# Attention features on two halves of 64 partitions, two heads in one pass of the array, and DRAM rows ordered by batch

## What is computed

```python
scores = einsum('bhqd,bhkd->bhqk', q, k) / sqrt(8)   # + bias, by core
attn = softmax(scores, axis=-1)
out = einsum('bhqk,bhkd->bhqd', attn, v)
```

## Time and profile before

| | |
|---|---|
| runs | 1136.57, 1138.33, 1139.11 us, median 1138.33 |
| profiled execution | span 1137.3 us from its first instruction to its last; no time of its own is given beside the span |
| busy | TensorE 866.6 us (76%), weight loads 548.7 (48%), DVE 652.5 (57%), ScalarE 517.1 (45%), GpSimd 155.7 (14%) |
| DMA | 80.82 MB in 109103 packets, 105280 of them under 2 KB; HBM read 49.61 MB, written 29.82 MB |
| chain that ended last | TensorE 62%, DVE 11%, DMA 7%, SyncE's queue 6%, issue 5% |

### The profile page before, as it was taken

The page is one execution under the profiler, slowest core; times in us unless marked ns, Lnnn a source line. Parts: engine busy times, 40 slices in busy tenths (PEclk is TensorE's granted clock), DMA queues, the critical chain, the costliest instruction groups (busy, mean ns, idle before and its releaser), DMA issues.

```text
span 1137.3 us, 21997 instructions
## 1 busy us (share of the span) xinstructions
PE 866.6 (76%) x7183; PEld 548.7 (48%) x7205; DVE 652.5 (57%) x1690; ACT 517.1 (45%) x867; POOL 155.7 (14%) x170
## 2 busy tenths in 40 slices
PE   6149998459999563856669998369999972899970
PEld 3015554325555332524425554235555552899970
DVE  5278884536666572535358884356656535455567
ACT  2216666515455531424416666414444541566640
POOL 5410000100000011000500000300000005502204
PEclk9659999659999886887659999779999985899995
DMA  4923332482223014100913330262212042212212
GB/s 164 245 75 58 57 57 90 139 125 45 54 46 98 1 41 91 34 1 29 194 37 63 63 62 1 73 104 44 44 34 37 15 165 93 77 46 63 68 40 72
DMA packets 109103, 80.82 MB, mean 71 GB/s; under 512 B 17344, under 2 KB 105280, under 8 KB 108112
## 3 DMA queue, kind: packets, MB, share of 16 engines
q1 hardware_dynamic: 105872, 69.73, 28.3%
q0 software_dynamic: 3168, 10.29, 2.6%
HBM read 49.61 MB, written 29.82 MB: 70 GB/s over the span
## 4 chain that ended last, share of the span: by engine, by line
PE 62%; DVE 11%; DMA 7%; SPq 6%; issue 5%; POOL 4%; ACT 4%; POOLq 0%; DVEq 0%; ACTq 0%
PE PS L447 11%; PE PS L423 10%; PE PS L405 9%; PE PS L1590 7%; PE PS L420 5%; PE PS L401 4%; PE PS L1600 3%; PE PS L459 3%; SPq L641 3%; DMA rows_q<-parts 3%; SPq L312 2%; DMA BIG<-MT 2%; PE PS L170 1%; POOL experts_x L1501 1%; DVE MS L581 1%
## 5 line engine op out<-in xcount | busy, mean ns | idle before, releaser
L581 DVE TENSOR_REDUCE MS<-PS 128x2 f32<-128x512 f32 (+1 forms) x544 | 340.5, 640 | 194.2 <-PE PS L423 190.8
L535 ACT ACTIVATE BIG<-PS 128x1024 f32<-128x1024 f32 (+2 forms) x288 | 260.3, 905 | 242.6 <-PE PS L405 241.1
L423 PE MATMUL PS<-BIG 96*128 96x256 bf16 (+1 forms) x1088 | 215.1, 283 | 49.4 <-DVE BIG L2136 36.1
L405 PE MATMUL PS<-BIG 128*128 128x256 bf16 (+1 forms) x1088 | 183.0, 268 | 6.9 <-DMA BIG<-MT 5.6
L447 PE MATMUL PS<-BIG,VA 128*32 128x256 f32 (+1 forms) x2176 | 163.4, 373 | 5.5 <-ACT OT L511 5.3
L423 PEld LDWEIGHTS PS<-BIG 96*128 96x128 bf16 x1088 | 99.9, 103 | 134.4 <-issue 65.9
L405 PEld LDWEIGHTS PS<-BIG 128*128 128x128 bf16 x1088 | 107.1, 99 | 40.2 <-issue 6.9
L1590 PE MATMUL PS<-OT,VA 128*128 128x128 f32 x736 | 96.6, 278 | 0.4 <-ACT OT L1647 0.4
L1590 PEld LDWEIGHTS PS<-OT,VA 128*128 128x128 f32 x736 | 91.3, 195 | 0.7 <-ACT OT L1647 0.7
L297 POOL TENSOR_TENSOR parts<-rbuf,parts 128x512 bf16<-128x512 f32 x34 | 40.1, 1186 | 263.0 <-ACT parts L222 262.7
L447 PEld LDWEIGHTS PS<-BIG,VA 128*32 128x32 f32 x2176 | 44.0, 108 | 60.5 <-issue 56.7
(11 more groups left out here) (220 smaller groups left out, 1058.6 us busy)
## 6 DMA issues: line engine op xcount, KB each, us to landing
BIG<-rows_q SPq DMA_DIRECT2D x64, 192.0 KB
rows_q<-parts SPq DMA_DIRECT2D x17, 384.0 KB, 3.3
rows_k<-parts SPq DMA_DIRECT2D x17, 384.0 KB, 2.7
BIG<-rows_k SPq DMA_DIRECT2D x64, 96.0 KB
BIG<-in_ex_w SPq DMA_DIRECT2D x3, 2048.0 KB, 11.8
rows_q<-parts SPq DMA_DIRECT2D x17, 256.0 KB, 3.3
BIG<-rows_k SPq DMA_DIRECT2D x64, 64.0 KB
OT<-experts_x SPq DMA_DIRECT2D x46, 64.0 KB, 1.8
```

The lines of the kernel that those rows point to most:

```text
L405: last = nc.tensor.matmul(bank[:, self.offset[kt]:self.offset[kt] + n], g.K6[b.par][:, h, kt * P:(kt + 1) * P], g.Q6[b.par][:, h, lo:lo + ...
L423: last = nc.tensor.matmul(bank[:, a, :], g.Q6[b.par][0:MROW, h, qt * P:(qt + 1) * P], g.K6[b.par][0:MROW, h, 0:kw], start=self.bias is Non ...
L535: nc.scalar.activation(g.PT[grp % 2][:, 2 * (u % 2):2 * (u % 2) + 2, 0:self.width], g.bank2[u % 2][:, :, 0:self.width], ACT.Exp, scale=SCALE)\
L581: nc.vector.reduce_max(g.MS[:, qt, 2 * pair:2 * pair + 2], g.bank[4 + v % 2][:, 0:2 * kw].rearrange("p (a k) -> p a k", a=2), axis=AX_X).t ...
```

## The change

The 48 feature rows of a head, the constant rows and the two rows of m now fit in 64 partitions: rows 0 to 47 the features, 48 to 61 constants, 62 and 63 m (`MROW = 62`). Heads u and u + 8 stand one above the other, on partitions 0 to 63 and 64 to 127, at the same place of the free dimension. `Q6` and `K6` become half as wide and have four buffers each instead of two, in the same memory.

- **TensorE** (`phase`): a phase has the maxima of head (u, a) of item `bm` and the scores of head (u, 1 - a) of item `be`, matmul by matmul in turn, each on its 64 rows of the array, in different banks. Maxima have one bank per head (both query tiles side by side). A bias comes behind the matmuls it is added to, and in the causal core only on the two diagonal blocks.
- The causal maxima are three blocks of 128 keys; DVE reduces them in one instruction, and a small `join` takes the smaller of the last two (the values are negated).
- `values` does both key tiles of four heads in one piece, once per group.
- **m's two parts** move from DVE to GpSimd; the sign is made by DVE's reduction (`negate=True`).
- **DRAM rows** are (batch, 24 rows, heads, tokens of a batch), written once for queries and keys alike, one DMA per batch. A load reads runs of 8 heads x 256 tokens, 4 KB, in three DMAs for the query and three for the key, for each half of the partitions: 12 per item, and 2 more for constants of the query in each buffer's first use or for the Gaussian rows. One semaphore covers the whole item.
- The constant rows of `K6` are the same for all cores and are loaded once, ones among them; the memsets and `const_rows_in` go.
- The hardware loops go; all steps are written out.

```diff
@@ class Split
+    def part(self, n, i):
+        return self.g.parts[n % NPARTS][:, i if self.jobs[n]["query"] else 2 - i, :]
@@ Split.sync
-            rows = j["to"].rearrange("(r d) h t -> (d h) r t", d=DH)[:, :, c * CH:(c + 1) * CH]
+            batches = CH // j["to"].shape[3]
+            rows = j["to"].rearrange("b (r d) h t -> b (d h) r t", d=DH)
             sp.wait_ge(*self.s3_ready.at(n + 1))
-            if j["query"]:
-                for first, k in ((0, 3), (3, 2), (5, 1)):
-                    sp.dma_start(rows[:, first:first + k, :], s[:, 3 - k, :].unsqueeze(1).to_broadcast([P, k, CH]))\
-                      .then_inc(self.written[n % NPARTS].sem, 16)
-            else:
-                sp.dma_start(rows, s[:, :, :]).then_inc(self.written[n % NPARTS].sem, 16)
+            w = CH // batches
+            for i in range(batches):
+                sp.dma_start(rows[c * batches + i], s[:, :, i * w:(i + 1) * w]).then_inc(self.written[n % NPARTS].sem, 16)
@@ Core.tensor
+        def maxima(b, u, a, qt, start):
+            rows = slice(64 * a, 64 * a + MROW)
+            first = P if self.causal and qt == 1 else qt * nqt * P
+            kw = P if self.causal and qt == 0 else nqt * P
+            return nc.tensor.matmul(g.bank[4 + a][:, first:first + kw], g.Q6[b.buf][rows, u, qt * P:(qt + 1) * P],
+                                    g.K6[b.buf][rows, u, 0:kw], start=start, stop=self.bias is None)
+        def scores(b, u, a, kt, start):
+            rows = slice(64 * a, 64 * a + 64)
+            lo, n = self.queries[kt]
+            return nc.tensor.matmul(g.bank[2 * (u % 2) + a][:, self.offset[kt]:self.offset[kt] + n],
+                                    g.K6[b.buf][rows, u, kt * P:(kt + 1) * P], g.Q6[b.buf][rows, u, lo:lo + n],
+                                    start=start, stop=self.bias is None)
+        def phase(bm, be, u, a):
+            if bm:
+                after(pe, self.mx_done, H * bm.no + 2 * u + a - 1)
+            for i in range(nqt):
+                start = self.bias is None or i == 0
+                if bm:
+                    mx = maxima(bm, u, a, nqt - 1 - i, start)
+                if be:
+                    st = scores(be, u, 1 - a, i, start)
+            if bm and self.bias is not None:
+                mx = add_bias(bm, g.bank[4 + a], False)
+            if be and self.bias is not None:
+                st = add_bias(be, g.bank[2 * (u % 2) + 1 - a], True)
...
+        def step(j, bm, be, bc):
+            for u in range(8):
+                heads(bm, be, u)
+                if u == 1:
+                    if be:
+                        after(pe, self.mts_done, self.m_turned)
+                        turn_m(be, 1)
+                    if bc:
+                        values(bc, 3)
+                elif u % 2 == 1 and be:
+                    values(be, u // 2 - 1)
+                if bm and u == 5:
+                    after(pe, self.mts_done, self.m_turned)
+                    turn_m(bm, 0)
+                if bc and u % 4 == 3 and u // 4 < nqt:
+                    turn_context(bc, u // 4)
@@ Core.vector, maxima(b, u)
+            n, w = self.mx_blocks, P if self.causal else nqt * P
+            for a in range(2):
+                dve.wait_ge(*self.mx_ready.at(H * b.no + 2 * u + a + 1))
+                nc.vector.tensor_reduce(g.MS[:, 0:n, a, u], g.bank[4 + a][:, 0:n * w].rearrange("p (n k) -> p n k", n=n),
+                                        axis=AX_X, op=ALU.max, negate=True).then_inc(self.mx_done.sem, 1)
@@ Core.gpsimd, parts_of_m(b, half)
+            t.done(nc.gpsimd.tensor_copy(parts[:, :, :, 0, :], m))
+            nc.gpsimd.tensor_tensor(parts[:, :, :, 1, :], m, parts[:, :, :, 0, :], ALU.subtract)\
+              .then_inc(self.mb_ready.sem, 1)
@@ Core.load
+        after(sp, self.st_ready, 8 * (b.no - NBUF + 1))
...
+            for a in range(2):
+                heads = src[b.no, :, 8 * a:8 * a + 8, :]
+                for first, lo, k in {"q": [(0, 0, 3 * DH), (3 * DH, 0, 2 * DH), (5 * DH, 0, DH)],
+                                     "k": [(0, 0, 3 * DH), (3 * DH, DH, 2 * DH), (5 * DH, 2 * DH, DH)],
+                                     "x": [(XROW, 0, self.xrows)]}[n]:
+                    sp.dma_start(to[64 * a + first:64 * a + first + k, :, 0:w], heads[lo:lo + k])\
+                      .then_inc(self.feat[b.buf].sem, 16)
```

More of the change, by code:

```diff
@@ L42 @@
 PARTS = 6
[L43 to L46 removed]
+XROW = PARTS * DH
+MROW = 62
+NBUF = 4
 NEG_CAUSAL = -1e30
@@ L200, in first_part @@
                 act.wait_ge(sem, before)
-            s1 = g.parts[n % NPARTS][:, 0, :]
+            s1 = self.part(n, 0)
             src = j.get("src")
@@ new lines, in scores, with add_bias @@
+        def scores(b, u, a, kt, start):
[4 more added lines that the diff above has]
+                                    start=start, stop=self.bias is None)
+        def add_bias(b, bank, transposed):
+            bias = self.bias_for(b, transposed)[:, 0:P if self.causal else nqt * nqt * P]
+            if self.causal:
+                bias = bias.unsqueeze(1).to_broadcast([P, 2, P])
+            return nc.tensor.matmul(self.biased(bank), g.ident_bf[:, :], bias, start=False, stop=True)
@@ L428, in turn_m, with heads @@
+        def heads(bm, be, u):
+            if bm and u == 0:
+                pe.wait_ge(*self.feat[bm.buf].at(bm.feat))
+            if be:
+                if u % 4 == 0:
+                    pe.wait_ge(*self.m_in[be.buf][u // 4].at((be.use + 1) * 32))
+                after(pe, self.exp_done, be.no * 8 + u - 1)
+            phase(bm, be, u, 0)
+            phase(bm, be, u, 1)
         def turn_m(b, half):
+            after(pe, self.cx_done, self.turned)
             pe.wait_ge(*self.mb_ready.at(b.no * 2 + half + 1))
@@ L502, in scalar @@
+        self.steps(step)
     def scalar(self, act):
@@ L541, in step @@
                     m_rows(bm, 0)
-                if self.tail and i is None:
+                if self.tail:
                     self.tail.run("scalar", act, (j, grp))
-        self.steps(act, step, self.nb - 1)
+        self.steps(step)
     def vector(self, dve):
@@ L591, in vector @@
-        body = self.steps
-        per = 2 * (2 + nqt)
-        def looped(j, i):
-            if i is not None and j == 2:
-                t.loop(i, per)
-            step(j, i)
-            if i is not None and j == 3:
-                t.end((self.nb - 2) // 2)
-        body(dve, looped, self.nb - 1)
+                    maxima(bm, u)
+                    if self.causal and u % 4 == 3:
+                        join(bm, u // 4)
+                if bc and u % 4 == 3 and u // 4 < nqt:
+                    context(bc, u // 4)
@@ L603, in gpsimd @@
+                if self.tail and u % 2 == 1:
+                    self.tail.run("vector", dve, (j, u // 2))
+        self.steps(step)
     def gpsimd(self, pool, values, ready, bias=None):
```

411 lines of the change are left out of this document (163 added, 248 removed).

## The result

The changed kernel takes **1121.2 us** (median of 4 runs, 1118.82 to 1122.65) where the kernel before takes 1137.75 beside it (4 runs, 1136.57 to 1139.11): a ratio of 0.9837, 95% interval 0.981 to 0.9865. It is faster, by 16.5 us. I had predicted 1095, 43 us less; the time measured lies inside the range that I had given, 1030 to 1130, but near its upper end. The profiled span is 1117.0 against 1137.3, so 20.3 us have to be found in the trace; the forecast's sum for the same span was 43.

A forecast was written before the change was run, and what follows sets the result against it. TensorE was taken to set the pace everywhere, DVE 2 us behind in the plain core. Terms -10 - 17 - 16 + 8 - 8 = -43 on a span of 1137.3 gave 1094.3, plus 1.0: 1095 us, range 1030 to 1130.

The forecast's parts named there:

- Two row tiles: TensorE phases: maxima and scores run side by side, four matmuls taking 0.22 us instead of 0.43.
- Switching: Biased phases: changing between row tiles and whole rows costs 0.10 us each way, 0.20 a phase.
- The first rival: Biased cores: tile switches cost little, so 0.20 us a phase goes; total 1021 to 1037; chance 0.22.
- Mask core: Core with the mask: 1.2 us less a step, about eight steps, -10 us.
- Causal core: Causal core: bias only on diagonal blocks, 2.1 us less a step, eight steps, -17 us.
- Plain core and the one behind the Gaussian: Cores without bias: DVE's work and waits make a step 13.0 us against 14.0, -16 us for both.
- The fourth rival: Whole kernel: m chain or SP's queue takes up what the tiles free; 1125 to 1137 us; chance 0.13.
- The m chain in the depths core: Depths core: waiting for m makes a step 10 us against 8.5, five steps, +8 us.
- The third rival: Plain steps: TensorE's clock falls to 1.2 GHz, 4.1 us more in 16 steps, kernel 1161 us; chance 0.03.
- GpSimd at price 0: m's two parts on GpSimd: under 1.2 us, hidden behind the next half's first two maxima, price 0.
- DMA and SP at price 0: SP's queue: 12 loads plus four m DMAs take 7.4 us of a 13 us step, price 0.
- Starts: Core starts: -4 us at the first core, -4 for the other four together, -8 in all.

The follow-up runs named there:

- e10: Changed kernel with the scores of a phase on the same 64 rows as its maxima, so no overlap: 1224.3 us, ratio 1.041 to the kernel before.
- e1: Changed kernel with values in two blocks of eight instructions in the two cores without a bias: ratio 0.9726 to the kernel before.
- e12: Changed kernel with m's two parts made by VectorE again instead of GpSimd: ratio 0.9854 to the kernel before.
- e7: Changed kernel with values in two blocks and SP's key and Gaussian loads moved behind m's second pair: 1087.67 us, ratio 0.9543 to the kernel before.
- e9: As e7, plus biases ahead of the row tiles in every second phase of mask and depths cores: 1111.21 us, ratio 0.9455 to the kernel before.
- e3: Changed kernel with the depths core's bias (causal masking) left out: depths core 50.1 us, one run.
- e6: Changed kernel with one more whole-array matmul of 256 columns in each depths core phase: depths core 71.3 us, one run.
- e11: Changed kernel with one more whole-array matmul of 512 columns in each depths core phase: depths core 63.1 us, one run.
- e5: Changed kernel with 60 whole-array matmuls of 512 columns run ahead of the depths core: depths core 61.2 us, one run.

## Why the prediction was wrong, point by point

The direction was right and the size was not: 16.5 us of 43. Two steps failed: the sum of DVE's work and waits in the cores without a bias (6.8 us), and the depths core, which I priced by the m chain at a clock that it did not get (13.6 us).

- **Two row tiles: right.** 0.22 for four; e10 prices them at 0.22 a phase and 73 us in all. At the efficiency that the Trainium skill states (TensorE: Matmul & The Clock Gate, Measured speedup vs the span model: four row tiles, 3.07 times) four would have taken 0.28 or 0.29, an estimate. The trace has 0.22, and no run here has four row tiles. That the sum of -22 by that estimate lies near the measured -20.3 is chance, since the miss is elsewhere.
- **Switching: right as a price**, 0.10 each way in every biased phase. The first rival is out.
- **Mask core: -9.3 for -10, by luck**, from two errors that cancel. The step was 0.5 shorter than forecast, but I multiplied by "about eight such steps", and eleven half steps are between the twelve contexts that stand at the steady distance.
- **Causal core: the factor was wrong.** The step of 14.6 came out exactly. But the eleven half steps between the steady contexts are five and a half steps and not eight: 11.3 us in all. The first and last steps gave 1.8 more, 13.1 measured, not 17.
- **Plain core and the one behind the Gaussian: "Sum 13.0 against 14.0" failed.** Both terms were too small. The eight reductions of a half step take 5.06 (2.52 and 2.54), not 8 x 0.585 = 4.68, since they start 0.61 apart and each four end in a whole 0.69: +0.4 a half step. DVE's waits on the values block are 1.45 a half step, where I had 1.15. The mechanism was named right ("values are now one block of 1.1 us") and e1 shows it, but its size took the whole gain. Of the 9.2 us that the two cores gained, 6.2 lie in their first and last steps, and 3.0 in single longer half steps that the kernel before had (7.35 to 8.19 beside 7.02). The fourth rival, *no gain in the pace*, came true here, though not by its means: neither the m chain nor SP's queue, but the block.
- **The m chain in the depths core: "10 against 8.5, five steps: +8" failed, and it is the largest part of the miss.** My 10 was the m chain's at a clock of 1.00. The clock stayed at 0.50, TensorE's own work became 12.27 a step, and in the steady steps the m chain did not matter: no wait for it there. It did in the first step, which I had not priced by itself and which holds 5.2 of the 21.6 us, 2.9 of them in the wait for m's first rows. I took the clock of the earlier trace rows over to a core whose work I was halving. The third rival had this mechanism, but looked for it in the plain cores, where the clock is 1.00, and used the depths core as evidence against.
- **GpSimd at price 0: right**, by e12, and so is its reverse: DVE had no use for the time.
- **DMA and SP at price 0: right at a step of 14**, and wrong as soon as the step is 12.4 (e1 against e7), and in first steps: by the waits of e7 this queue holds m's first rows for 3.5 us in the causal core and 2.1 in the depths core. How much of that a core gets back differs (4.4 us in e7's causal core, 1.5 in e9's; 3.3 in e7's depths core).
- **Starts: -11.2 for -8.** The first gave 7.6 instead of 4, since DVE's large memsets are gone and the first maxima start at 48.35 instead of being held until 69.37, with DVE's own work on the rows and two smaller memsets up to 62.4 as the next bound; the other four together -3.6 for -4.

By the sum: depths 13.6, plain cores 6.8, causal 3.9, mask 0.7, the last stage 0.9, less 3.2 from the starts, is 22.7 us, the whole distance from -43 to -20.3.

Not tried: undoing the order of the rows in DRAM, or the three blocks of the causal maxima. What the depths core would take at 1.00 without a filler stays an estimate, and so does what about its work holds the clock down. e3, e6 and e10 stayed at 0.50 and e11 did not; they differ in more than one thing.

## What to carry to other kernels

When an engine is made faster, look at the longest block that it now issues between two results for the next engine, and compare it with what that engine has buffered: here 1.07 us of values stood against two banks, and splitting the block (with the loads moved around it) gave 29 us where the whole change had given 20. Count the steps in which all stages of a pipeline overlap before multiplying, price the first step of each stage by itself, and re-read the clock for each stage whose work on TensorE shrinks: here the stage with the shortest matmuls stayed at 1.2 GHz throughout and lost 21.6 us.

## What the runs showed of the hardware that I had not expected

- A busy share of 8.00 of 8 us in the profile is no sign of a full clock. The depths core was at 0.50 with it, in e5 too, where it had started at 1.00, and in e6; it went to 1.00 in e11. More work then ran in nearly the same time: 63.1 against 61.5 us.
- An accumulation begun by a whole-array bias and ended by row tiles runs like the other order; the seams are equal both ways, 0.09 to 0.11.
- One DMA costs SP's queue 0.37 us (six in 2.25) to 0.5 (six in 3.05), so fourteen in a row hold it for 6 us. The small transfer of m's first rows stood 3.1 us behind such loads in the depths core, from 429.9 to 433.0.
